# A feed-forward stage quantised to FP4: GpSimd passes in pieces, norms on ScalarE, another order on VectorE

## The reference

```python
def fp4_quant_dequant(x):                       # blocks of 16 along the last dim
    xb = x.reshape(shape[:-1] + (shape[-1] // 16, 16))
    scale = jnp.maximum(jnp.max(jnp.abs(xb), axis=-1, keepdims=True) / 6.0, 1e-12)
    xn = xb / scale
    q = _GRID[jnp.searchsorted(_MID, jnp.abs(xn))] * jnp.sign(xn) * scale
    return q.reshape(shape)

def _L1_ffn_ref(x, w_gate, w_up, w_down):       # weights 704x256, 704x256, 256x704
    gate = fp4_linear(x, w_gate)                # fp4_linear quantises both of its inputs
    y = fp4_linear(x, w_up)
    h = jax.nn.silu(gate) * y
    return fp4_linear(h, w_down)

x = x + _layernorm(_L1_attn_ref(_layernorm(x), ...))      # the scan; x3 in the kernel
x = x + _layernorm(_L1_ffn_ref(_layernorm(x), w_gate, w_up, w_down))
```

## Time and profile before

| | |
|---|---|
| three runs, us | 4414.91, 4418.63, 4428.33 (median 4418.63) |
| the profiled execution, us | 4417.65, its span 4415.9 |
| busy over the span | PE 3440.4 (78%), DVE 3356.8 (76%), ACT 2000.7 (45%), POOL 1533.5 (35%) |
| weights of the stage | from 3846 us, last GpSimd pass to 3889.9 |
| the stage itself | first y at 3899.6, last out addition to 4412.6 |

### The profile page before, as it was taken

How to read it: one execution, slowest core, us unless ns; L and a number is a source line. 1 busy time by engine, 2 the same in 40 slices (tenths; PEclk the granted TensorE clock), 3 DMA queues, 4 the chain that set the end, 5 groups by cost and what they waited for, 6 DMA issues and landing times. The chain is left out here.

```text
span 4415.9 us, 59241 instructions
## 1 busy us (share of the span) xinstructions
PE 3440.4 (78%) x16346; PEld 1457.5 (33%) x16347; DVE 3356.8 (76%) x4871; ACT 2000.7 (45%) x2475; POOL 1533.5 (35%) x882
## 2 busy tenths in 40 slices
PE   4859999999999999697996586616667677557765
PEld 1413333323323333274664332201111111145654
DVE  5758888888888888153443489938888988779998
ACT  0406676666666666430113565514444444223322
POOL 0110000000000000041007235648899998734544
PEclk7959999999999999768997698857777777678887
DMA  1640101011010100322223424341111111211110
GB/s 48 232 119 3 41 3 43 3 42 25 21 41 4 42 3 5 134 101 77 65 61 118 148 92 138 128 113 58 58 58 58 59 58 58 75 38 46 39 37 12
DMA packets 234477, 276.38 MB, mean 63 GB/s; under 512 B 42953, under 2 KB 189650, under 8 KB 232914
## 3 DMA queue, kind: packets, MB, share of 16 engines
q1 hardware_dynamic: 217490, 240.93, 17.9%
q0 software_dynamic: 6144, 17.05, 1.2%
q10 hardware_dynamic: 10688, 16.32, 1.1%
HBM read 153.48 MB, written 120.37 MB: 62 GB/s over the span
## 5 line engine op out<-in xcount | busy, mean ns | idle before, releaser
L885 DVE TENSOR_REDUCE att_maxima<-att_ps_m 128x1 f32<-128x512 f32 x2048 | 1280.4, 682 | 259.9 <-PE att_ps_m L928 256.2
L859 ACT ACTIVATE att_probs<-att_ps_s 128x1024 f32<-128x1024 f32 x1024 | 996.2, 1021 | 442.7 <-PE att_ps_s L942 440.0
L928 PE MATMUL att_ps_m<-att_ks,att_qs 96*128 (+1 forms) x2048 | 730.2, 392 | 46.7 <-DMA att_ks<-scratch_k 28.8
L942 PE MATMUL att_ps_s<-att_qs,att_ks 99*128 (+1 forms) x2048 | 612.5, 381 | 23.8 <-DMA att_qs<-att_m_parts 21.7
L2177 POOL TENSOR_TENSOR ss_ch<-ss_h,ss_c_rep 128x1024 f32<-128x1024 f32 x256 | 594.7, 2350 | 2.4 <-DVE ss_h L2223 2.2
L950 PE MATMUL att_ps_o<-att_probs,att_vs 128*32 128x512 f32 x4096 | 546.7, 606 | 0.4 <-ACT att_probs L859 0.4
L2198 ACT ACTIVATE ss_ps_d<-ss_ps_d,ss_a_neg 128x1024 f32<-128x1024 f32 x256 | 278.6, 1088 | 515.9 <-PE ss_ps_d L2263 515.8
L928 PEld LDWEIGHTS att_ps_m<-att_ks,att_qs 96*128 (+1 forms) x2048 | 165.2, 97 | 640.4 <-DVE att_maxima L885 367.2
L2285 PE MATMUL ss_ps_y<-ss_ch,ss_sum_block 128*32 128x256 f32 x2048 | 216.4, 507 | 144.7 <-POOL ss_ch L2177 144.7
L2255 PE MATMUL ss_ps_x<-ss_stack,ss_spread 96*128 96x512 bf16 x512 | 204.6, 491 | 147.2 <-ACT ss_skip L2186 74.9
L2223 DVE TENSOR_TENSOR_SCAN ss_h<-ss_ps_d,ss_u 128x1024 f32<-128x1024 f32 x128 | 289.2, 2277 | 29.7 <-ACT ss_ps_d L2198 15.0
(11 more groups left out here) (408 smaller groups left out, 5198.5 us busy)
## 6 DMA issues: line engine op xcount, KB each, us to landing
scratch_steps<-si_parts SPq DMA_DIRECT2D x48, 512.0 KB, 5.7
ss_stack<-scratch_steps SPq DMA_DIRECT2D x256, 96.0 KB
att_qs<-scratch_q SPq DMA_DIRECT2D x192, 64.0 KB
ex_x<-scratch_sorted_x SPq DMA_DIRECT2D x72, 132.0 KB, 2.0
scratch_sorted_y<-ex_y SPq DMA_DIRECT2D x72, 128.0 KB, 1.7
scratch_v<-qkv_v_ext SPq DMA_DIRECT2D x8, 1024.0 KB, 4.4
att_vs<-scratch_v SPq DMA_DIRECT2D x8, 1024.0 KB
moe_w_w<-in_W ACTq DMA_DIRECT2D x16, 512.0 KB, 12.3
```

Source lines behind the costliest of these rows:

```text
L859: act.activation(probs[:, (2 * kt + pair) % 4, :, :], ps_s[pair][:, :, :], ACT.Exp, scale=HD ** -0.5).then_inc(exp_done, 1)
L885: dve.tensor_reduce(maxima[:, j, c:c + 1], ps_m[BANK[j * QC + c]][:, :], AX.X, ALU.max).then_inc(maxed, 1)
L928: pe.matmul(ps_m[BANK[j * QC + c]][:, :], q, k, start=True, stop=True).then_inc(scored, 1)
L942: mm = pe.matmul(ps_s[pair][:, i, :], ks[0:ROWS, bass.ds(st // QC % 2, 1), h, kt * P:(kt + 1) * P], qs[0:ROWS, bass.ds(st // QC % 2, 1), b ...
```

## The change

- In `fp4_weights` and in all GpSimd passes of `fp4_ffn` one instruction over the whole tile becomes several over pieces: quarters of 384 for a third of the weights, pieces of 352 (half of a tile's 704) for h, 256 (one tile) for x. A pass over h is four instructions, a pass over x two.
- The statistics are combined by one `bn_aggr` for each of the 6 columns instead of the seven operations of `ln_var`. eps is added as the bias of ScalarE's Ln, and the reciprocal root is refined in three operations and a fourth that makes -mean x rstd.
- z, xf and v are made on ScalarE, as activations with scale and bias, in three new stages behind its first take of gate and up.
- VectorE's order is new, make_h stands ahead of make_x3 and make_x, and make_out is last. The former `all_rstd` is two stages, `variances` and `scales`, with split_xq between. All of VectorE's steps are unrolled.

The orders of the other engines are those of before, but for the new stages on ScalarE. The core of the diff:

```diff
@@ fp4_weights, gpsimd
-                    pool.tensor_tensor(q, q, m, ALU.subtract).then_inc(pool_steps, 1)
-                    pool.wait_ge(pool_steps, piece + 1)
-                    pool.tensor_tensor(x, q, over(scales.unsqueeze(2), [P, PIECE // FP4, FP4]), ALU.mult).then_inc(quantised, 1)
+                    for b in quarters(PIECE // FP4):
+                        pool.tensor_tensor(q[:, b, :], q[:, b, :], m[:, b, :], ALU.subtract).then_inc(pool_steps, 1)
+                    for n, b in enumerate(quarters(PIECE // FP4)):
+                        pool.wait_ge(pool_steps, piece * QUARTERS + n + 1)
+                        ins = pool.tensor_tensor(x[:, b, :], q[:, b, :], over(scales[:, b].unsqueeze(2), [P, PIECE // FP4 // QUARTERS, FP4]), ALU.mult)
+                    ins.then_inc(quantised, 1)
@@ fp4_ffn, vector
+                def variances(step, parity):
...
+                    for n in range(NT):
+                        dve.bn_aggr(moments[:, n, :], st[:, n, :]).then_inc(s["var_ready"], 1)
+
+                def scales(step, parity):
+
+                    c = Chain(dve, s["rstd_steps"], step * NEWTON)
+                    dve.wait_ge(s["rstd_ready"], step + 1)
+                    c.then(dve.scalar_tensor_tensor(newton[:, :], r0[:, :], -0.5, r0[:, :], ALU.mult, ALU.mult))
+                    c.wait()
+                    c.then(dve.scalar_tensor_tensor(newton[:, :], var, EPS, newton[:, :], ALU.add, ALU.mult))
+                    c.wait()
+                    c.then(dve.scalar_tensor_tensor(rstd[:, :], newton[:, :], 1.5, r0[:, :], ALU.add, ALU.mult))
+                    c.wait()
+                    dve.scalar_tensor_tensor(nmr[:, :], mean, -1.0, rstd[:, :], ALU.mult, ALU.mult).then_inc(s["scale_ready"], 1)
...
                 def make_x3(u, slot):
-                    c = Chain(dve, s["z_steps"], u * UT)
-                    for k in range(UT):
-                        c.then(normed(dve, z[:, k, :], y[:, k, :], ln, k))
-                    c.wait()
+                    dve.wait_ge(s["z_ready"], (u + 1) * UT)
...
-                run_stages(dve, UNITS4, (stats_out, 5), (add_xm, 0), (stats_x3, 1), (split_xq, 2), (all_rstd, 0, STEPS4), (make_out, 5),
-                           (make_x, 1), (make_x3, 0), (make_h, 3))
+                run_stages(dve, UNITS4, (stats_out, 5), (add_xm, 0), (stats_x3, 1), (variances, 0, STEPS4), (split_xq, 2), (scales, 0, STEPS4),
+                           (make_h, 3), (make_x3, 0), (make_x, 1), (make_out, 5), unroll=True)
@@ fp4_ffn, gpsimd
                     pool.wait_ge(s["gu_taken"], (u + 1) * UT * 6)
-                    pool.tensor_tensor(up[:, slot, :, :], up[:, slot, :, :], gate[:, slot, :, :], ALU.mult).then_inc(s["gu_product"], 1)
+                    for k in range(UT):
+                        for f in halves(FFN):
+                            pool.tensor_tensor(up[:, slot, k, f], up[:, slot, k, f], gate[:, slot, k, f], ALU.mult).then_inc(s["gu_product"], 1)
...
+                    for k in range(UT):
+                        for f in halves(FFN):
+                            pool.tensor_tensor(h_round[:, k, f], h_round[:, k, f], h_magic[:, k, f], ALU.subtract).then_inc(s["hq_steps"], 1)
                     pool.wait_ge(s["hq_turned"], u * UT * 2)
                     for k in range(UT):
...
+                        for i, f in enumerate(halves(FFN)):
+                            pool.wait_ge(s["hq_steps"], (u * UT + k) * 2 + i + 1)
+                            at, n = k * HB // UT + f.start // FP4, FFN // 2 // FP4
+                            ins = pool.tensor_tensor(in_blocks(hq[:, k, f]), in_blocks(h_round[:, k, f]),
+                                                     over(h_scale[:, at:at + n].unsqueeze(2), [P, n, FP4]), ALU.mult)
                     ins.then_inc(s["hq_ready"], 1)
@@ fp4_ffn, scalar
+                def scale(out, x, n):
+                    return act.activation(out, x, ACT.Identity, bias=nmr[:, n:n + 1], scale=rstd[:, n:n + 1])
+
+                def scale_y(u, slot):
+                    act.wait_ge(s["scale_ready"], u + 1)
+                    act.wait_ge(s["x3_ready"], u)
+                    for k in range(UT):
+                        scale(z[:, k, :], y[:, k, :], k).then_inc(s["z_ready"], 1)
...
-                run_stages(act, UNITS4, (copy_x, 2), (all_rstd, 0, STEPS4), (first_tile(take_gu), 2), (first_tile(copy_h), 4), (second_tile(take_gu), 2),
-                           (second_tile(copy_h), 4), (sigmoid, 2))
+                act.wait_ge(s["padded"], 3)
+                run_stages(act, UNITS4, (copy_x, 2), (all_rstd, 0, STEPS4), (first_tile(take_gu), 2), (scale_y, 0), (scale_x3, 1), (scale_out, 5),
+                           (first_tile(copy_h), 4), (second_tile(take_gu), 2), (second_tile(copy_h), 4), (sigmoid, 2))
```

More of the change, by code:

```diff
@@ L2342, with quarters, halves, in_blocks @@
 FP4_STEPS = 6
+QUARTERS = 4
+def quarters(n):
+    return [slice(i * n // QUARTERS, (i + 1) * n // QUARTERS) for i in range(QUARTERS)]
+def halves(n):
+    return slice(0, n // 2), slice(n // 2, n)
+def in_blocks(ap):
+    return ap.rearrange("p (b k) -> p b k", k=FP4)
 def blocks_of(ap):
@@ L2497, in fp4_ffn @@
         STEPS4 = UNITS4 + BEHIND[-1]
-        ln = LnScratch(r, "ln", NORMS * UT)
+        NT = NORMS * UT
+        st, moments = r.sb("ln_stats", [P, NT, 6]), r.sb("ln_moments", [P, NT, 2])
+        eps = r.sb("ln_eps", [P, 1])
+        lnv, r0, newton, rstd, nmr = (r.sb("ln_" + n, [P, NT]) for n in ("lnv", "r0", "newton", "rstd", "nmr"))
+        mean, var = (moments[:, :, i:i + 1].rearrange("p n o -> p (n o)") for i in range(2))
         ps_p, ps_x, ps_o = r.ps("ps_p", [P, UT, C]), r.ps("ps_x", [P, UT, KC, P]), r.ps("ps_o", [P, UT, C])
@@ L2577, in make_x @@
                 def make_x(u, slot):
-                    c = Chain(dve, s["x_steps"], u * X_STEPS)
-                    for k in range(UT):
-                        c.then(normed(dve, xf[:, k, :], x3[:, bass.ds(u * UT + k, 1), :].rearrange("p o c -> p (o c)"), ln, UT + k))
-                    c.wait()
+                    c = Chain(dve, s["x_steps"], u * FP4_STEPS)
+                    dve.wait_ge(s["xf_ready"], (u + 1) * UT)
                     x, m, q = blocks_of(xf[:, :, :]), blocks_of(x_magic[:, :, :]), blocks_of(x_round[:, :, :])
@@ L2596, in make_h @@
                     fp4_round(dve, c, x, h_inv[:, :], m, q).then_inc(s["h_rounded"], 1)
-                    assert c.n == H_STEPS, c.n
+                    assert c.n == FP4_STEPS, c.n
                 def make_out(u, slot):
-                    c = Chain(dve, s["o_steps"], u * UT)
-                    for k in range(UT):
-                        c.then(normed(dve, v[:, k, :], ps_o[:, k, :], ln, 2 * UT + k))
-                    c.wait()
-                    dve.sem_inc(s["o_taken"], 1)
+                    dve.wait_ge(s["o_taken"], (u + 1) * UT)
                     dve.wait_ge(out_stored[slot], (u // 2 + 1) * 16)
@@ L2630, in scale_x @@
                     pool.wait_ge(s["x_rounded"], u + 1)
-                    pool.tensor_tensor(q, q, m, ALU.subtract).then_inc(s["q_steps"], 1)
-                    pool.wait_ge(s["q_steps"], u + 1)
+                    for k in range(UT):
+                        pool.tensor_tensor(x_round[:, k, :], x_round[:, k, :], x_magic[:, k, :], ALU.subtract).then_inc(s["q_steps"], 1)
                     pool.wait_ge(s["xq_turned"], u)
-                    pool.tensor_tensor(blocks_of(xq[:, :, :]), q, over(x_scale[:, :].unsqueeze(2), [P, XB, FP4]), ALU.mult).then_inc(s["xq_ready"], 1)
+                    for k in range(UT):
+                        pool.wait_ge(s["q_steps"], u * UT + k + 1)
+                        ins = pool.tensor_tensor(in_blocks(xq[:, k, :]), in_blocks(x_round[:, k, :]),
+                                                 over(x_scale[:, k * XB // UT:(k + 1) * XB // UT].unsqueeze(2), [P, XB // UT, FP4]), ALU.mult)
@@ L2636, in scale_h @@
+                    ins.then_inc(s["xq_ready"], 1)
                 def scale_h(u, slot):
-                    m, q = blocks_of(h_magic[:, :, :]), blocks_of(h_round[:, :, :])
                     pool.wait_ge(s["h_rounded"], u + 1)
-                    pool.tensor_tensor(q, q, m, ALU.subtract).then_inc(s["hq_steps"], 1)
-                    pool.wait_ge(s["hq_steps"], u + 1)
+                    for k in range(UT):
+                        for f in halves(FFN):
+                            pool.tensor_tensor(h_round[:, k, f], h_round[:, k, f], h_magic[:, k, f], ALU.subtract).then_inc(s["hq_steps"], 1)
@@ L2657, in all_rstd, with scale_x3, scale_out @@
                 def all_rstd(step, parity):
-                    ln_act(act, ln, step, s["var_ready"], s["ln_ready"], s["rstd_ready"])
+                    act.wait_ge(s["var_ready"], (step + 1) * NT)
+                    act.activation(lnv[:, :], var, ACT.Ln, bias=eps[:, 0:1]).then_inc(s["ln_ready"], 1)
+                    act.wait_ge(s["ln_ready"], step + 1)
```

(16 more changed lines are left out.)

35 lines of the change are left out of this document (14 added, 21 removed).

## The result

| | before | after |
|---|---|---|
| median of the runs compared, us | 4418.77 (5 runs) | 4397.59 (5 runs, 4384.34 to 4400.28) |
| profiled execution, us (its span) | 4417.65 (4415.9) | 4400.28 (4398.5) |
| ratio of the times | | 0.9942, 95% interval 0.9925 to 0.9958 |

The medians differ by 21.2 us, 0.5%; the ratio over all runs gives 0.6%. The forecast was 4416 with a range from 4398 to 4440, and no change by over 0.3% as the likeliest outcome. It was wrong: the time lies 0.4 us under the range.

The account below looks back on a forecast made before the run. VectorE sets the pace before; after, a VectorE-GpSimd ring: 12.1 + 16.5 + 0.16 + 0.1 + 0.4 = 29.3 us a step against 29.6. The span ends 2.7 earlier, own time 4414.95, median 4416, range 4398 to 4440.

Parts of the forecast that it names:

- The start: Feed-forward stage up to x(2) rounded, forecast at 3964.1, from the old first take at 3931.23 coming 1.9 later.
- The ring: VectorE and GpSimd wait for each other each step; period is VectorE's 12.1 plus all GpSimd passes, 29.3 us in all.
- The 1.9 us of delay: First take of gate and up comes later by 0.9 for the weights and 1.0 for round trips to ScalarE.
- The pieces, less the two waits that they save: GpSimd's 13 more passes a step add 2.1 us; two multiplies no longer waiting for a subtraction save 0.2.
- The port: GpSimd standing while VectorE's out additions and 6-element operations run: 0.4 us a step, bounds 0 and 1.5.
- The tail: After x(15) rounded at 4345.0: last products and h of units 14 and 15, to 4395.3, then 17.9 us.
- (a): Rival: VectorE stays the bound and sheds stalls and norms, some 20 us a step, 4295; chance 4%.
- (b): Rival: a piece's fixed part hides behind the piece before and the port costs nothing; period 26.8, 4384; chance 8%.
- (c): Rival: GpSimd stands in full for VectorE's two-input operations; period 30.4 to 31.4, taken as 4438; chance 20%.
- the last third grows by 0.9: Weights: the last third, which nothing hides, grows by 6 x 0.15 = 0.9 us from the pieces.
- What would have shown the prediction right: GpSimd idle some 12 us, make_h undisturbed, VectorE waiting 4 or more for h, pieces near 0.95, period 29.3.
- What would have shown it wrong: Period under 28.5 or over 30.2, or VectorE's long waits ended by ScalarE's z, TensorE's ps_o or a load.

Follow-up runs that it names:

- e3: Kernel before with make_x3 ahead of make_x in VectorE's order and nothing else: median 4414.21 us, ratio 0.997.
- e2: Changed kernel with make_x ahead of make_x3 in VectorE's order: median 4401.8 us, ratio 0.9959 to the kernel before.
- e1: Changed kernel with GpSimd's feed-forward passes whole again, the weights keeping their pieces: median 4376.12 us, ratio 0.9905 to the kernel before.
- e4: Changed kernel with VectorE's order of before (make_out, make_x, make_x3, make_h): median 4438.17 us, ratio 1.0037 to the kernel before.
- e5: Changed kernel with whole feed-forward passes and times_up ahead of scale_x on GpSimd: median 4380.36 us, ratio 0.9893 to the kernel before.
- e7: Changed kernel with the norms z and xf back on VectorE, v staying on ScalarE: median 4423.67 us, ratio 1.0000 to the kernel before.
- e9: e1 with make_h, scale_h and what follows them one step later: median 4379.57 us, ratio 0.9899 to the kernel before.
- e10: Changed kernel with each h pass in eight pieces of 176 instead of four of 352: median 4438.55 us, ratio 1.0047 to the kernel before.
- e11: e1 with the weights' passes whole too: median 4374.85 us, ratio 0.9888 to the kernel before.
- e6: Kernel before with only the pieces in GpSimd's feed-forward passes: median 4398.39 us, ratio 0.995.

## Why the prediction was wrong

The forecast for the profiled execution was a span end of 4413.2; it was 4398.5. The 14.7 us go as follows.

| step of the prediction | predicted | measured | difference, us |
|---|---|---|---|
| stage start to x(2) rounded | 3964.1 | 3956.26 | -7.8 |
| thirteen periods | 13 x 29.3 | 13 x 28.62 | -8.8 |
| x(15) rounded to the last hq | 50.3 | 52.3 | +2.0 |
| last hq to the end of the span | 17.9 | 17.9 | 0 |

**The start failed as a mechanism.** The prediction took the first take of gate "which began at 3931.23" as fixed, later by 1.9 for what the change puts ahead of it. It came at 3926.23, 6.9 sooner than that. That time was not set by x but by the load that TensorE's projection waits for, 5.07 us, and the change moves the x3 sum, and so that load, ahead of make_x. The rival to this reading, that the start gained by the new norms or by the unrolled loop, falls by e3: the swap alone, with none of these, brings the first take to 26.13 us after the first y, and after has 26.04. The 1.9 us of delay hardly showed either: the pieces of the weights cost 0.2 us and not 0.9 (below), and with the norms on ScalarE and x first as in before (e2) the take comes 30.5 us after the first y, 1.1 sooner than in before and not 1.0 later. Why it does stays open. The row that told it, TensorE's projection with its DMA wait, stood ahead of the gate rows that I read. The prediction did weigh the earlier x3 sum for the steady steps (wanted 7 us later, nearly tight) and left it out at the start, where it was late.

**The ring was right, and its terms were a little large.** In seven variants the period came out within 0.3 us of what was worked out before it ran, from the two orders and the measured step of after (e1, e2, e4, e5, e7, e9, e10), and VectorE's part is the forecast's to 0.03. GpSimd's side was taken as 16.5, with 0.4 for the port, 0.1 for the loop and 0.16 for handovers, 17.2 together. It measured 16.58 with the port in it, and 0.11 for handovers, 16.7. The failing step is this sum; every term of it was a little too high:

- The pieces, less the two waits that they save, were taken as 2.1 - 0.2 = 1.9 and cost 1.7 (e1).
- The port was taken as 0.4. x_round with both out additions beside it starts the next pass 1.67 later, where one with neither beside it (at 3934.24, same kernel) lasts 1.41: some 0.3.
- The loop's end shows in no row, and each handover took 0.08 or less.

(The step shown takes 28.76; the mean over thirteen is 0.14 less, since the first two take 28.4 and the last 28.0.) Thirteen times 0.68 us is 8.8 us of the result. The term for the port had its price from the z norm, "0.08 of its 0.41 us". That reading is incomplete: the norm ended 0.25 us after x_round had begun, so no more than 0.25 could be lost to it. These rows of after, each a VectorE operation and the piece beside it, give the measure:

```profile
4128.21 0.95 DVE L2633 TENSOR_TENSOR fp_o<-fp_v,fp_x 128x256 f32<-128x256 f32 x1
4128.84 0.90 POOL L2661 TENSOR_TENSOR fp_x_round<-fp_x_round,fp_x_magic 128x256 f32<-128x256 f32 x1
```

```profile
4352.39 2.23 DVE L2339 SCALAR_TENSOR_TENSOR fp_h_round<-fp_h_round,fp_h_magic 128x1408 f32<-128x1408 f32 x1
4353.10 2.30 POOL L2645 TENSOR_TENSOR fp_up<-fp_up,fp_gate 128x352 f32<-128x352 f32 x1
```

The first piece takes 0.73 without such an operation beside it, the second 0.93. The operations end 0.32 and 1.52 after the piece has begun, and the pieces are longer by 0.17 and 1.37: the overlap less 0.15. For the z norm it is 0.25 and 0.08 (rows 3 and 6: 1.37 for 1.29). So GpSimd did stand for VectorE's operation, but for the overlap alone and less some 0.15.

**The tail was too short.** The forecast priced the last times_up at 3.6 us and make_h(14) at 7.8, each undisturbed, but they run beside each other:

```profile
4349.13 6.28 POOL L2645 TENSOR_TENSOR fp_up<-fp_up,fp_gate 128x352 f32<-128x352 f32 x4 [4.19 <-ACT fp_up L2726]
```

```profile
4349.26 1.55 DVE L2335 TENSOR_SCALAR fp_h_magic<-fp_h_round 128x1408 int32<-128x1408 int32 x1
4350.85 1.51 DVE L2337 TENSOR_SCALAR fp_h_magic<-fp_h_magic 128x1408 f32<-128x1408 f32 x1
4352.39 2.23 DVE L2339 SCALAR_TENSOR_TENSOR fp_h_round<-fp_h_round,fp_h_magic 128x1408 f32<-128x1408 f32 x1
```

Four pieces with VectorE's operations let in between take 6.28 us, and make_h 9.7. The product started 20.8 us after x(15) was rounded, forecast 22.0, so 2.7 - 1.2 of the 2.0 are the product's. The rest, 0.5, is h_round and hq of units 14 and 15, 6.9 and 6.8 us instead of 6.6 each. make_h(14)'s own 9.7 cost nothing, for it ended beside the product.

**The rivals.** (a) is out: VectorE did shed its work (27.6 to 20.2) and the time did not follow, for it turned the work into a wait of 7.5 us. (b), pieces that cost nothing, is out by e1 and e10. (c) is out at its price: its period was 30.4 or more. Its mechanism is there, as the rows above show, but the two out additions cost 0.3, where it has 2 x 0.41. Of the weights, "the last third grows by 0.9": its two GpSimd passes take 3.86 and 3.23 us instead of 3.45 and 2.81. That VectorE's stalls there stay within 0.5 us was wrong in the good direction, its second and third thirds taking 10.17 and 10.74 us instead of 11.78 each. From the first third rounded to the last GpSimd pass the pieces cost 0.2 us (30.2 instead of 30.0), and e11 against e1 shows no difference in the whole time beyond the intervals. What would have shown the prediction right, all of it was seen but the period: GpSimd idle 12.18, make_h undisturbed, a wait of 7.50 for h, pieces of 0.90. What would have shown it wrong was not seen: the period of 28.62 is not under 28.5. Half of the miss came from the start, for which no sign was given.

**What stays open.** The medians differ by 21.2 us, the profiled executions by 17.4. The remaining 3.8 is within what executions of one kernel differ by; after's five runs span 16 us. The place of that variation, ahead of the stage, was not looked into. VectorE's unrolled loop, the bn_aggr and the third norm (v) on ScalarE were not tried by themselves; e3 and e6 have none of them, the other runs all three.

## What to carry to other kernels

Where two engines hand work back and forth, write their new orders side by side before counting busy time: here each waited for the other once a step, and the sum of the two parts gave the period of every variant that kept that ring. Splitting a pass helps only where the engine held up by it is the bound; in a ring of waits each piece is paid in full. Here the best version undid the pieces and kept the order and the norms, so try the parts of a change by themselves: the pieces alone looked like all of its gain. Before a time of the old trace is carried over as fixed, ask what released it, one engine further back than the row itself.
